# Scores in 32-row products, an earlier mix, and one product per tile of the path's one-hot

## The reference

```python
# cross attention: 16 heads of 16, one key and one value head shared by all
q = layernorm(x) @ Wq + bq;  k = ctx @ Wk + bk;  v = ctx @ Wv + bv
scores = where(mask == 0, -1e9, q_h . k / sqrt(16))
x = x + concat_h(softmax(scores) @ v) @ Wo + bo
# feed-forward over the sequence
z = layernorm(x)
m = k0 * z[t-1] + k1 * z[t] + k2 * z[t+1]           # mix of neighbouring rows
h = m @ W1[p] + b1[p];  path[p] = h @ W2[p] + b2[p]  # 9 paths, 64 wide
best = argmax(tanh(m @ Wo1 + bo1) @ Wo2 + bo2)
out = x + layernorm(z + path[best]) * gamma + beta
```

## Time and profile before

| | us |
|---|---|
| median of 3 runs | 399.1 |
| the runs | 394.74, 399.10, 399.69 |
| the profiled execution | 399.22 |
| its span, first to last instruction | 397.1 |
| TensorE, VectorE, ScalarE, GpSimd busy | 346.2, 298.8, 182.3, 196.6 |
| mean granted clock of TensorE | 0.968 |

### The profile page before, as it was taken

One profiled execution on the slowest core, in us unless ns is written; L12 is line 12 of the kernel. 1 busy time (PEld: TensorE's weight loads), 2 busy tenths in 40 slices (PEclk: granted clock), 3 DMA queues, 4 the chain that ended last, 5 costly groups with the idle time before them and its releaser, 6 DMA issues.

```text
span 397.1 us, 7274 instructions
## 1 busy us (share of the span) xinstructions
PE 346.2 (87%) x2636; PEld 279.6 (70%) x2636; DVE 298.8 (75%) x647; ACT 182.3 (46%) x271; POOL 196.6 (50%) x235
## 2 busy tenths in 40 slices
PE   1866984984999999999899999999899999889990
PEld 0745774764877987788577976797588877866890
DVE  3667298498579764789899836889888795699867
ACT  1442725632655366435745374436651455146400
POOL 2640103334206449843939179726944397239234
PEclk9995997999899999999999999999999999999997
DMA  7333452301130004201140105010300110001003
GB/s 209 99 128 95 87 122 72 74 2 26 25 98 1 18 11 111 67 2 26 63 109 0 26 0 172 0 26 0 107 2 0 29 53 2 2 0 54 1 2 106
DMA packets 24004, 20.10 MB, mean 51 GB/s; under 512 B 10593, under 2 KB 20650, under 8 KB 23978
## 3 DMA queue, kind: packets, MB, share of 16 engines
q1 hardware_dynamic: 22338, 19.18, 18.1%
q10 hardware_dynamic: 1640, 0.57, 0.6%
HBM read 9.26 MB, written 4.19 MB: 34 GB/s over the span
## 4 chain that ended last, share of the span: by engine, by line
PE 56%; DVE 21%; issue 13%; ACT 3%; POOL 3%; DMA 2%; SPq 0%; DVEq 0%; POOLq 0%; ACTq 0%
PE ps L429 8%; PE ps L569 5%; PE ps L434 4%; PE ps L652 4%; PE ps L634 4%; PE ps L657 4%; PE ps L653 4%; PE ps L503 3%; PE ps L529 3%; PE ps L530 3%; PE ps L559 3%; PE ps L532 2%; DVE mx L1094 2%; DVE st L1038 2%; PE ps L544 2%
## 5 line engine op out<-in xcount | busy, mean ns | idle before, releaser
L1399 POOL TENSOR_TENSOR rs<-ve,halfneg 128x4 f32<-128x4 f32 x24 | 25.3, 1052 | 154.1 <-DVE ve L1054 154.0
L1087 DVE SCALAR_TENSOR_TENSOR ql<-ps,bqs,qh 64x512 fp32r<-64x512 f32 x32 | 24.0, 750 | 30.7 <-ACT qh L807 30.3
L820 ACT ACTIVATE e<-ps 128x1024 f32<-128x1024 f32 x32 | 32.9, 1027 | 19.8 <-PE ps L532 19.8
L1094 DVE TENSOR_REDUCE mx<-ps 128x16 f32<-128x1024 f32 x32 | 37.9, 1214 | 2.5 <-PE ps L503 2.5
L652 PE MATMUL ps<-w2h,hmh 128*128 128x256 f32 (+1 forms) x140 | 35.1, 286 | 0.0
L653 PE MATMUL ps<-w2l,hmh 128*128 128x256 f32 (+1 forms) x140 | 34.4, 281 | 0.0
L1444 POOL TENSOR_TENSOR hml<-hs,hmh 128x512 fp32r<-128x512 f32 x24 | 30.1, 1271 | 6.5 <-ACT hmh L874 6.5
L569 PE MATMUL ps<-wo,osb 128*128 128x256 f32 x128 | 30.8, 386 | 1.7 <-DVE osb L1112 1.7
L429 PE MATMUL ps<-xmh,w1h 128*128 128x512 f32 x80 | 26.9, 417 | 5.9 <-ACT xmh L845 5.4
L1433 POOL TENSOR_TENSOR y<-xh2f,gms 128x256 f32<-128x256 f32 x28 | 23.6, 872 | 13.4 <-DVE xh2f L1063 13.4
L864 ACT ACTIVATE hs<-ps,b1s 128x512 f32<-128x512 f32 x28 | 19.3, 688 | 23.4 <-PE ps L434 23.1
(11 more groups left out here) (156 smaller groups left out, 884.8 us busy)
## 6 DMA issues: line engine op xcount, KB each, us to landing
xin<-in_x SPq DMA_DIRECT2D x8, 512.0 KB, 3.9
qh<-mT SPq DMA_DIRECT2D x16, 256.0 KB, 3.8
out<-y SPq DMA_DIRECT2D x7, 512.0 KB, 3.1
ql<-thT SPq DMA_DIRECT2D x16, 128.0 KB, 2.4
min_<-in_mask_Bx1xSxS_ik SPq DMA_DIRECT2D x8, 128.0 KB, 3.8
cst<-in_constants SPq DMA_DIRECT2D x1, 768.0 KB, 6.9
cst<-in_constants SPq DMA_DIRECT2D x1, 660.5 KB, 6.0
hs<-in_L_ffn_W SPq DMA_DIRECT2D x2, 288.0 KB
```

The lines of the kernel that those rows point to most:

```text
L820: nc.scalar.activation(e[:, 2 * i:2 * i + 2, :], ps[:, bank:bank + 2, :], ACT.Exp).then_inc(s_e, 1)
L1094: v.tensor_reduce(mx[:, k, :].rearrange("p (a h) -> p a h", a=2), ps[:, bank:bank + 2, :].rearrange("p a (h s) -> p a h s", s=SK), AX.X, A ...
```

## The change

**Scores.** The maxima come from `scores_for_max` with q rounded to fp32r (`q_round`, VectorE), split in two halves of 64 rows that go to different banks, on top of a bf16 product that adds the mask. `scores_transposed` runs in two passes t, one before and one after `wq`. Each has, for four groups g of 32 rows (two heads each), a product in plain fp32 of the unsplit q with the keys (`kst`), then mask products in bf16 with 64 rows, then products of the maxima, in bf16 halves (`split_max`, `nm`, `nmT`), with 32 rows. `q_copy` on ScalarE writes q once. `qh`, `ql`, `kmh`, `kml`, `kms` and the DMAs `place_mask` and `place_maxima` go; GpSimd's `operands` becomes two multiplications.

**Mix.** `early_mix(b)` mixes all but the last column of chunk 0 in the step with n = (b, 1), on VectorE between `q_round` and `argmax`; ScalarE's `early_mixed_hi` follows `onehot_copy` and `mixed_hi`, GpSimd's `early_mixed_lo` stands before `selected_lo`. `last_column` adds the missing column late in that step, before `x_lo`. In the step (0,1) both stand at its end, and on ScalarE behind `copy_t2`.

**Path.** `onehot_transposed` transposes `oh` once, `onehot_copy` (ScalarE) brings it to SBUF, and `rep` is one bf16 product of 10 rows by 512 columns per m. `rep(0)` comes after `spread` instead of before it. The feed-forward's banks have one use more (`ohT`).

The core of the diff (setup, semaphores' names and the removed operand code left out):

```diff
-                for q in range(NQ):
-                    bank = banks[k % 2] + q // 2
-                    mm = nc.tensor.matmul(ps[:, bank, (q % 2) * 256:(q % 2 + 1) * 256],
-                                          qh[:, q, k * P:(k + 1) * P], kmh[:, q % 2, :],
-                                          start=True, stop=True)
+                ks = slice(k * P, (k + 1) * P)
+                bank = banks[k % 2]
+                for a in range(2):
+                    r = half_rows(a)
+                    nc.tensor.matmul(ps[:, bank + a, :], mT[r, j, ks], mask_ident[r, :], start=True, stop=False)
+                for m in range(KD):
+                    for a in range(2):
+                        r = half_rows(a)
+                        mm = nc.tensor.matmul(ps[:, bank + a, m * 256:(m + 1) * 256], qr[r, m, ks], kmx[r, :],
+                                              start=False, stop=(m == KD - 1))
                 mm.then_inc(s_sn, 1)
...
-                for p in range(NPAIR):
-                    q, c = p // 2, slice((p % 2) * P, (p % 2 + 1) * P)
-                    bank = 2 + p % 4
-                    if p >= 4 and p % 2 == 0:
-                        pe.wait_ge(s_e, at(b, NJ * 4, j * 4 + p // 2 - 1))
-                    nc.tensor.matmul(ps[:, bank, :], kmh[:, q % 2, c], qh[:, q, :], start=True, stop=False)
-                    nc.tensor.matmul(ps[:, bank, :], kml[:, q % 2, c], qh[:, q, :], start=False, stop=False)
-                    nc.tensor.matmul(ps[:, bank, :], kms[:, q, c], ql[:, q, :],
+            def scores_transposed(b, j, t, front):
+                if t == 0:
+                    if front:
+                        pe.wait_ge(s_mT, at(b, NJ, j + 2))
+                    pe.wait_ge(s_q, at(b, NJ * KD, (j + 1) * KD))
+                    pe.wait_ge(s_km, at(b, 3, 2))
+                    pe.wait_ge(s_mx, at(b, NJ * NT, (j + 1) * NT))
+                for g in range(4):
+                    if t and g % 2 == 0:
+                        pe.wait_ge(s_e, at(b, NJ * 4, j * 4 + g // 2 + 1))
+                    nc.tensor.matmul(ps[:, 2 + g, :], kst[quarter(g), :], q[quarter(g), t, :], start=True, stop=False)
+                for g in (0, 2, 1, 3):
+                    r = half_rows(g // 2)
+                    nc.tensor.matmul(ps[:, 2 + g, :], mask_ident[r, 0:P], mT[r, j, :], start=False, stop=False)
+                if t == 0:
+                    pe.wait_ge(s_nT, at(b, NJ, j + 1))
+                for g in range(4):
+                    nc.tensor.matmul(ps[:, 2 + g, :], max_rows[quarter(g), t * P:(t + 1) * P], nmT[quarter(g), :],
                                      start=False, stop=True).then_inc(s_st, 1)
...
+            def onehot_transposed(b, j, L=usual):
+                o = take_slot(b, j, "ohT", L)[0:NPATH + 1, 0:CH // 2].bitcast(BF16)
+                pe.wait_ge(s_oh, at(b, NJ, j + 1))
+                for k in range(NT):
+                    mm = nc.tensor.transpose(o[:, k * P:(k + 1) * P], oh[:, k, :], ident_b[:, :])
+                mm.then_inc(L.s_f, 1)
             def rep(b, j, m, L=usual):
                 o = take_slot(b, j, f"rep{m}", L)
                 if m == 0:
-                    pe.wait_ge(s_oh, at(b, NJ, j + 1))
-                for k in range(NT):
-                    ks = slice(k * P, (k + 1) * P)
-                    for a in range(2):
-                        p = 2 * m + a
-                        if p < NPATH:
-                            sel = oh[:, k, p:p + 1].broadcast_to([P, DM])
-                            mm = nc.tensor.matmul(o[a * DM:(a + 1) * DM, ks], sel, ident_b[:, :], start=True, stop=True)
-                        else:
-                            mm = nc.tensor.matmul(o[DM:DM + NPATH, ks], oh[:, k, 0:NPATH], ident_b[:, :],
-                                                  start=True, stop=True)
-                mm.then_inc(L.s_f, 1)
+                    pe.wait_ge(L.s_fa, L.read_by_act(b, j, NFA))
+                r = rows_of(m)
+                nc.tensor.matmul(o[0:r, :], path_rows[0:NPATH + 1, m * P:m * P + r], ohT[0:NPATH + 1, :],
+                                 start=True, stop=True).then_inc(L.s_f, 1)
...
                 if n:
-                    scores_transposed(*n, front)
+                    scores_transposed(*n, 0, front)
                 if front:
                     wq(*front, fb)
+                if n:
+                    scores_transposed(*n, 1, front)
...
-                    rep(*f, 0)
+                    onehot_transposed(*f)
                 elif front:
                     scores_for_max(*front, 0, banks)
                     scores_for_max(*front, 1, banks)
                 if n:
                     spread(*n)
                 if f:
+                    rep(*f, 0)
...
+                    nc.scalar.activation(q[:, m, :], ps[:, bank + m, :], ACT.Identity, bias=bqs[:, m:m + 1]).then_inc(s_q, 1)
...
+            def onehot_copy(b, j, L=usual):
+                act.wait_ge(L.s_f, L.filled(b, j, "ohT"))
+                nc.scalar.activation(ohT[0:NPATH + 1, :], ps[0:NPATH + 1, L.bank(j, "ohT"), 0:CH // 2].bitcast(BF16),
+                                     ACT.Copy).then_inc(L.s_fa, 1)
...
+                    onehot_copy(*f)
                 if f and f[1] == 0:
                     mixed_hi(f[0], 1)
+                if f and n[1] == NJ - 1:
+                    early_mixed_hi(n[0])
...
+                if n and n[1] == NJ - 1 and not f:
+                    early_mixed_hi(n[0])
...
+            def q_round(b, j):
+                for m in range(KD):
+                    dve.wait_ge(s_q, at(b, NJ * KD, j * KD + m + 1))
+                    a = v.tensor_copy(qr[:, m, :], q[:, m, :])
+                a.then_inc(s_qr, 1)
...
+                maxima = mx[:, :, :].rearrange("p k (r h) -> p k r h", r=1).broadcast_to([P, NT, 4, H])
+                v.tensor_copy(nm[:, :, :, 0:H], maxima).then_inc(s_nmh, 1)
+                v.tensor_tensor(nm[:, :, :, H:2 * H], maxima, nm[:, :, :, 0:H], ALU.subtract).then_inc(s_nm, 1)
...
+            def last_column(b):
+                col = slice(CH - 1, CH)
+                dve.wait_ge(s_x2T, at(b, NJ * KD, NJ * KD))
+                v.tensor_tensor(edge[:, :, :], x2T[:, :, CH - 1:CH + 2], mks[:, :, :].rearrange("p t c -> p c t"),
+                                ALU.mult).then_inc(s_edge, 1)
+                dve.wait_ge(s_edge, b + 1)
+                v.tensor_reduce(xm[:, :, col], edge[:, :, :], AX.X, ALU.add).then_inc(s_xm, KD)
+                dve.wait_ge(s_xm, at(b, NJ * KD, KD))
+                v.tensor_copy(xmh[:, :, col], xm[:, :, col]).then_inc(s_xmh, KD)
+                dve.wait_ge(s_xmh, at(b, NJ * KD, KD))
+                dve.wait_ge(s_earlyl, at(b, KD, KD))
+                v.tensor_tensor(xml[:, :, col], xm[:, :, col], xmh[:, :, col].bitcast(F32), ALU.subtract).then_inc(s_xml, KD)
...
-                if front and n:
-                    q_lo(*front, 0 if f else 6)
+                if front:
+                    q_round(*front)
                 if f and f[1] == 0:
-                    mix(f[0], 1)
-                if n and not front:
+                    second_mix(f[0])
+                if f and n[1] == NJ - 1:
                     early_mix(n[0])
...
+                if f and n[1] == NJ - 1:
+                    last_column(n[0])
                 if n and not front:
-                    mix(n[0], 0, CH - 1)
-                    mixed_lo(n[0], 0, CH - 1)
-                if f:
-                    residual_stats(*f, 1)
-                if n and not front:
-                    mix(n[0], 1)
+                    second_mix(n[0])
                 if after:
                     x_lo(*after, 0 if f else 6)
                 if f:
                     layernorm3_apply(*f)
-                if n and n[1] == NJ - 1 and front:
-                    if not f:
-                        dve.wait_ge(s_wf, 16 * WF_LOADS)
-                    mix(n[0], 0)
-                    mixed_lo(n[0], 0)
+                elif n and n[1] == NJ - 1:
+                    dve.wait_ge(s_wf, 16 * WF_LOADS)
+                    early_mix(n[0])
+                    last_column(n[0])
...
+            def early_mixed_lo(b):
+                for c in range(KD):
+                    pool.wait_ge(s_earlyh, at(b, KD, c + 1))
+                    js = slice(0, CH - 1)
+                    g.tensor_tensor(xml[:, c, js], xm[:, c, js], xmh[:, c, js].bitcast(F32), ALU.subtract).then_inc(s_earlyl, 1)
```

290 lines of the change are left out of this document (119 added, 171 removed).

## The result

The changed kernel takes 404.3 us (median of 5 runs, 402.9 to 407.2) against 399.7 us before (5 runs): 1.0147 times as long, 95% interval 1.0088 to 1.0207 (the ratio goes by the means, 404.7 and 398.7). The forecast was 392.5, in a range up to 404.0; the sign came out the other way. The profiled execution has a span of 405.4 us against 397.1; at 407.2 us it is the slowest of the five.

A forecast was written before the change was run, and what follows sets the result against it. The prediction took TensorE savings to count only where nothing else is late next, with VectorE's chain level with TensorE behind spread. Its terms for launch, steps and tail summed to -6.65 us from 399.2, forecast 392.5, range 380 to 404.

The forecast's parts named there:

- The step that failed: Steady steps, with TensorE's products priced at full clock: even steps 42.2 us, odd ones 41.3.
- Scores: Score products: two passes of 1.8 us each, 3.6 a step in place of 5.7, a gain of 2.1.
- Rival (c): Score passes: the row groups don't overlap, a pass takes 5.2 us, 438 us in all; chance 0.07.
- Rival (b): Score passes: changes between 32-row and 64-row products empty the array, 0.4 us each, 407 us; chance 0.12.
- First half: From a step's start to the end of spread: 23.35 us in (2,0), 1.9 gained, and 22.4 in (1,1).
- Second half: From the end of spread to the next step, mostly VectorE's chain: 18.9 us against 19.2.
- Cost of the spreading: Path spreading: 2.5 us a step becomes five products of 0.22 and four transposes, 1.2 us less work.
- Launch: Launch to step (0,0): -1.0 us as a wait for q_lo goes; removing mask and maxima placements changes nothing.
- (1,0): Step (1,0): +1.2 us, as the exponentials stand behind early_mixed_hi on ScalarE and start near +5.
- (0,1): Step (0,1): -1.4 us, as q_lo leaves VectorE, less what split_max and later exponentials take back.
- (3,1): Step (3,1), with no wq between the passes: +0.8 us, from rep0 behind spread and early_mixed_lo on GpSimd.
- Rival (a): Whole kernel: TensorE is the real bound and VectorE only echoes it, -29 us, 370 us; chance 0.16.

The follow-up runs named there:

- e13: The changed kernel with the product that spreads the path over 128 rows in place of 10, other rows zero: 397.9 us, ratio 0.9991.
- e14: e11 with its eleven path products a step over 128 rows in place of 10: 398.8 us, ratio 0.9984.
- e7: e2 with the four gamma multiplications of the output moved from GpSimd to VectorE: 398.3 us, ratio 1.0013.
- e5: The kernel before with only the scores in 32-row groups, mixing and path spreading as before: 407.8 us, ratio 1.0247.
- e4: The kernel before with only the transposed one-hot and its 10-row path product: 401.7 us, ratio 1.0067.
- e1: The changed kernel with SyncE's later loads held until the first mask transpose is copied, as before: 401.7 us, ratio 1.0072.
- e12: The kernel before with SyncE's five later loads issued ahead of the first mask placement: 400.6 us, ratio 1.0062.
- e2: The changed kernel with score products for the maxima and a path product repeated in the waits behind spread: 398.6 us, ratio 0.9995.
- e9: The changed kernel with loads held, repeated products, q copied early, gamma on VectorE and reordered ends: 384.9 us, ratio 0.9681.
- e10: e9 without any repeated product, otherwise the same instructions in the same order: 386.3 us, ratio 0.9679.
- e11: e2 with its filler changed: score products done once, 10-row path tile 1 six times: 411.4 us, ratio 1.0299.
- e8: e2 with the first w1 tile between the score passes of (3,1) and a w2 tile moved in the tail: 399.1 us, ratio 1.0031.

## Why the prediction was wrong

**The step that failed** is the one that set the expected lengths of the steady steps: every product behind step (1,0) was priced at full clock. The prediction named the case in its last paragraph ("a granted clock below 1.0 within steady steps, from TensorE's new idle time, would make me wrong as well"), but gave it no place, price or chance, although it had worked out 2.6 us of new idle time in the first half of a step, and 1.6 us less work in the second. The runs showed 27 us at half clock from (1,1) on, where before had none, and that this hangs on the form of the path product (e13, e14). e13 shows what the rest of the working was worth, as it is the changed kernel with the clock kept but for one stretch in the tail. Differences of the profiled executions to before, in us:

| | launch | (0,0) | (0,1) | (1,0) | (1,1) | (2,0) | (2,1) | (3,0) | (3,1) | tail | sum |
|---|---|---|---|---|---|---|---|---|---|---|---|
| forecast | -1.0 | -1.25 | -1.4 | +1.2 | -0.3 | -2.2 | -0.3 | -1.9 | +0.8 | -0.3 | -6.65 |
| changed | +1.3 | -1.5 | -2.4 | +0.5 | +2.4 | -0.6 | +1.0 | -0.1 | +4.1 | +3.5 | +8.3 |
| e13 | -0.3 | -1.5 | -2.4 | +0.5 | +0.9 | -2.4 | +1.0 | -1.8 | +0.8 | +0.2 | -5.1 |

Of the 13.4 us between the two profiles 1.6 are the launch, which differs by as much between profiles of one code; nearly all of the other 11.8 lie in the five parts that have stretches at 0.50. But these profiles are extremes: the changed kernel's is the slowest of its five executions, e13's (393.8 us) the fastest of its ten. By the medians the forecast was missed by 11.8 us, and the form of the path product accounts for 6.4 of them. Of the 5.4 us by which e13's median, 397.9, still lies above the forecast, some 2.4 may be clock as well. That is an estimate: the median of its executions' mean clocks is 0.956, in the profile it is 0.962, and 0.006 of 396 us is 2.4 us. No profile of such an execution was kept, and the rest stays open. So the gain of 6.65 us that the working promised is borne out by the fastest execution of e13, not by its typical one (ratio to before 0.9991).

**Scores.** A pass took 2.0 us in place of 1.8. The set of four 32-row products, which was to stay within 0.9 us, took 1.14, the length that the prediction had named beside its sum (1.13) and not used. All behind it took 0.92 us, changes of shape included, against 0.96. Rival (c) is refuted. Rival (b), changes of row shape at 0.4 us each, gave 407 and would seem confirmed by the time alone; the pass refutes it, since it would have lasted 2.7 us. A time that agrees proves nothing about a mechanism.

**First half.** `spread` ended at +23.2 in (2,0) (23.35 forecast) and +22.7 in (1,1) (22.4), the wait before h1 was 0.8 us (1.5 expected) and that before `wq` 0.95 (1.0).

**Second half.** 18.9 us were forecast; (2,1), at full clock, has 19.4. `attn_normalise` starts 1.4 to 1.8 us behind `spread` in place of 1.0, since VectorE waits up to 1.24 us for x, whose load is issued when GpSimd lets go of the buffer (201.68 in (2,0)) and lands 3.7 us later; I had left that DMA out. Removing that wait in e7 gave back 0.3 to 0.5 us a step. These 0.5 us and the 0.3 of the first half are what (2,1), 42.1 us, has over the 41.3 forecast for an odd step.

**Cost of the spreading.** I priced the ten-row product by its columns, 0.22 us, and that was right. What it replaced, 2.5 us a step of products over 128 rows, seems to have done something that no row of busy time shows: it kept the clock up behind `spread`. The odd steps of e5, which still have these products, kept their clock; in e4, without them, only (3,0) of the full steps lost it. So it takes the other parts of the change too to lose it in (1,1) and (2,0), and which of them was not isolated.

**Launch.** "No row had an engine waiting for them, so nothing" was wrong of the mask placement. It had itself been a wait on SyncE's queue, and the loads behind it were late for it; without it they compete with ScalarE's (e1, e12). The step -1.0 came out +1.3, of which the competition is about 2.

**(1,0)** +0.5 instead of +1.2, and (0,1) -2.4 instead of -1.4; the sum of both was -1.9 against -0.2 forecast, and which terms made the difference was not worked out. The exponentials of (1,0) did start 4.6 us into the step, near the +5 forecast. **(3,1)** was right by e13 (+0.8); the other 3.3 us in the changed kernel come with its stretch at 0.50.

**Rival (a)** (TensorE is the bound, 370 us) is refuted from the other side: (2,1) has 1.1 us more work in e2 than in the changed kernel and the same length, and so it is with e9 and e10 (0.9 us in (2,0)). Its price was also too high: it counted six full steps and then (3,1) again, but there are five; with them it comes to about 374.

## What to carry to other kernels

Where a change takes work from TensorE or makes its products narrower, list the places in which it will stand idle or run products over few rows afterwards, and price the work behind each at both clock levels. The 512-column product over ten rows cost as much time as the one over 128, and where the other rows can hold zeros at no cost the wide form is the safer one. When two kernels differ by a per cent, compare the clocks of all their executions, not two profiles. And a wait on a DMA queue that nobody waits for may still be what keeps the loads behind it out of the way.

## What the runs showed of the hardware that was not expected

- A bf16 product of 512 columns takes 0.38 to 0.39 us as shown alone, over 10 rows as over 128. With the 10-row form the granted clock fell to 0.50 among eleven of them, with no wait of TensorE between (e11, from 210.5 on); with the 128-row form at the same places it did not (e14). Times of whole kernels: 411.4 against 398.8, and 404.3 against 397.9.
- Repeated work made a kernel faster: 1.1 us more in a full step, 5.7 us less in the total (e2 against the changed kernel).
- The same passage fell to 0.50 in one kernel's profile and not in that of another with the same instructions there (the tail of e2 and e8, step (2,1) of the changed kernel and of e1), so a single profile is not the last word on it.
- 1.5 MB more on the DMA engines in the first 16 us made a 256 KB load land 2.3 us later.
